# Reordering the slots of a software-pipelined attention and FFN kernel, and moving its last output step from VectorE to ScalarE and GpSimd

## The reference, cut to what matters

```python
# layer 1, per sequence
ifg = concat([q, k, v]); ig = ifg @ igate_w.T + igate_b; fg = ifg @ fgate_w.T + fgate_b
log_D = tril(cumsum(log_sigmoid(fg))[s] - cumsum(...)[t]) + ig[t]
D_mat = exp(log_D - max_t(log_D))
C = (q_h @ k_h.T / sqrt(16)) * D_mat
h = (C / (maximum(abs(C.sum()), exp(-max_log_D)) + 1e-6)) @ v_h
x1 = x + layernorm(h) * ln_scale
# layer 2
y = concat([n, -n]) with n = layernorm(x1)
out = x1 + s2 * (relu2(s1 * (relu2(s0 * (y @ W0)) @ W1)) @ W2)      # W: 128(256)->512->512->128, relu2 = 2*relu
```

## Time and profile before

| what | value |
|---|---|
| time before, median of 3 runs | 140.13 us (139.77 to 140.87) |
| the profiled execution's own time | 140.68 us |
| its span | 138.9 us |
| PE busy | 112.5 us, 81% |
| DVE busy | 95.9 us, 69% |
| ACT busy | 74.7 us, 54% |
| POOL busy | 70.0 us, 50% |
| mean granted TensorE clock | 0.956 of full |

### The profile page before, as it was taken

One profiled execution on the slowest core, in us unless ns is written; L12 is line 12 of the kernel. 1 busy time (PEld: TensorE's weight loads), 2 busy tenths in 40 slices (PEclk: granted clock), 3 DMA queues, 4 the chain that ended last, 5 costly groups with the idle time before them and its releaser, 6 DMA issues. The chain is left out here.

```text
span 138.9 us, 3358 instructions
## 1 busy us (share of the span) xinstructions
PE 112.5 (81%) x1141; PEld 83.7 (60%) x1141; DVE 95.9 (69%) x294; ACT 74.7 (54%) x173; POOL 70.0 (50%) x143
## 2 busy tenths in 40 slices
PE   4899999993998299979969698698888858769861
PEld 4777668562955185575827467376474656658751
DVE  5685595879689685809994994985898546471631
ACT  3026675974676464379649717835744631374230
POOL 5592675188784786654665777553214032520000
PEclk9999999999599959999999999999999977999997
DMA  3482190149683774635284753737001000101001
GB/s 104 138 224 49 39 258 15 42 60 183 121 151 61 161 132 66 134 54 101 19 189 76 156 105 88 147 38 159 2 5 38 0 5 0 38 0 38 17 26 38
DMA packets 12992, 11.38 MB, mean 82 GB/s; under 512 B 2080, under 2 KB 11440, under 8 KB 12976
## 3 DMA queue, kind: packets, MB, share of 16 engines
q0 software_dynamic: 1728, 6.29, 25.3%
q1 hardware_dynamic: 10112, 4.53, 12.7%
q10 hardware_dynamic: 1136, 0.35, 1.0%
HBM read 8.94 MB, written 1.25 MB: 73 GB/s over the span
## 5 line engine op out<-in xcount | busy, mean ns | idle before, releaser
L453 PE MATMUL pF<-h,w 128*128 128x256 f16 x256 | 31.1, 277 | 0.0
L643 ACT ACTIVATE h<-pF 128x512 f16<-128x512 f32 x32 | 18.1, 594 | 22.9 <-PE pF L453 22.9
L870 DVE SCALAR_TENSOR_TENSOR h<-pF,h 128x512 f16<-128x512 f32 x32 | 21.1, 681 | 9.5 <-ACT h L643 9.5
L453 PEld LDWEIGHTS pF<-h,w 128*128 128x128 f16 x256 | 25.1, 100 | 3.1
L1017 POOL TENSOR_SCALAR ve_hx<-mv_hx 128x2 f32<-128x2 f32 (+1 forms) x17 | 4.0, 236 | 32.8 <-DVE mv_hx L828 31.7
L783 DVE SCALAR_TENSOR_TENSOR cmat<-pS,dmat 128x1024 f32<-128x1024 f32 x15 | 18.2, 1216 | 2.1 <-PE pS L379 2.1
L379 PE MATMUL pS<-q_heads,qcT 64*128 64x512 f32 x64 | 18.1, 641 | 0.3 <-DVE cmat L783 0.3
L996 POOL TENSOR_SCALAR_AFFINE_SELECT maxb<-aT 128x1024 f32<-128x1024 f32 x12 | 13.2, 1102 | 4.4 <-ACT em L573 4.4
L412 PE MATMUL pX<-ident,x2p 128*128 128x128 f16 x32 | 4.4, 217 | 13.6 <-POOL x2p L1029 13.4
L796 DVE SCALAR_TENSOR_TENSOR den<-pO,em 128x8 f32<-128x8 f32 x16 | 2.6, 164 | 17.1 <-PE pO L400 17.1
L1018 POOL TENSOR_TENSOR rs_hx<-ve_hx,minus_half 128x2 f32<-128x2 f32 (+1 forms) x17 | 13.0, 766 | 1.4
(11 more groups left out here) (124 smaller groups left out, 211.5 us busy)
## 6 DMA issues: line engine op xcount, KB each, us to landing
maxb<-running_max POOLq DMA_DIRECT2D x12, 512.0 KB, 5.3
out<-outb SPq DMA_DIRECT2D x8, 128.0 KB, 1.8
xs<-in_x SPq DMA_DIRECT2D x3, 256.0 KB, 7.2
cs_in<-in_ctx SPq DMA_DIRECT2D x3, 256.0 KB, 7.6
q_heads<-qcT SPq DMA_DIRECT2D x24, 32.0 KB, 2.7
xs<-in_x SPq DMA_DIRECT2D x2, 128.0 KB, 3.2
cs_in<-in_ctx ACTq DMA_DIRECT2D x1, 256.0 KB, 3.7
k_in<-in_L_ffn_k SPq DMA_DIRECT2D x1, 256.0 KB, 3.8
```

Source lines behind the costliest of these rows:

```text
L453: last = pe.matmul(bank[:, u], w1[:, k, columns], h1[:, k, part], start=(k == 0 and part == 0), stop=(k == FT - 1 and part == 1))
L643: act.activation(hidden(f, m, 0), ffn_place(f, m), ACT.Relu).then_inc(ffn_high, 1)
L870: dve.scalar_tensor_tensor(out=hidden(f, m, 1), in0=ffn_place(f, m), scalar=0.0, in1=hidden(f, m, 0), op0=ALU.max, op1=ALU.subtract).then_ ...
```

## The change

It has these parts:

- PE's slot: `turn_o(n-1)` goes ahead of the early FFN stage, `turn_late_xn` behind it; `spread_never`/`spread_max` go ahead of `turn_x2`; `keep_busy` (slots 3 to 5) has two products in place of five and stands ahead of `turn_o`.
- POOL's slot: `x2_take_low(n-4)` stays first, `hx_scale(n-1)` follows it (so each scaling comes one slot later than before, and ahead of `place`), then `place`, `take_values`, and the new `add_out` in slots whose early stage is LAST.
- DVE's slot: only the first `low` of the late stages is ahead of `make_c`, the second is behind it; `residual` and `x_statistics` come right after, then the scans, `norm_q`, `x_moments`, and the normalizer chain in one piece. `norm_group(2)` goes from the end of slot 1 to the place ahead of its gate scans.
- The output: ACT scales the last product from PSUM into a new buffer `out_x` in SBUF, POOL adds x1 to it; DVE's instruction for it goes. PE's wait for the bank is on ACT's copy (`out_scaled`).
- SP waits for the first group of ctx and the second of x before it issues the loads of the third groups.

```diff
@@ sync
             load_ctx(1)
+            sp.wait_ge(ctx_loaded[0], 16)
+            sp.wait_ge(x_loaded[1], 16)
             load_x(2)
@@ tensor, ffn
-                        pe.wait_ge(out_ready, f_before + 1)
+                        pe.wait_ge(out_scaled, f_before + 1)
@@ tensor, slot
                     weigh(n - 1)
-                if 0 <= n - 4 < B:
-                    turn_x2(n - 4)
-                if k == 3 and g + 2 < NG:
-                    turn_late_xn(g + 2)
-                for f, m in early:
-                    ffn(f, m)
                 if 2 <= n + 1 < DIRECT:
                     spread_never(n + 1)
                     spread_max(n + 1, 0)
                     spread_max(n + 1, 1)
+                if 0 <= n - 4 < B:
+                    turn_x2(n - 4)
+                if 3 <= n <= FFN_LAG:
+                    pe.wait_ge(exp_ready, DIRECT)
+                    keep_busy(2)
                 if 0 <= n - 1 < B:
                     turn_o(n - 1)
+                for f, m in early:
+                    ffn(f, m)
+                if k == 3 and g + 2 < NG:
+                    turn_late_xn(g + 2)
                 for f, m in late:
                     ffn(f, m)
                 if n == 1:
                     turn_am(1)
-                if 3 <= n <= FFN_LAG:
-                    pe.wait_ge(exp_ready, DIRECT)
-                    keep_busy(5)
@@ scalar, high
+                act.wait_ge(ffn_sums, sums_to(f, m))
                 if m == LAST:
+                    if f >= 2:
+                        act.wait_ge(out_ready, f - 1)
+                    act.activation(out_x[:, f % 2].rearrange("p j d -> p (j d)"), ffn_place(f, m)[:, 0], ACT.Copy,
+                                   scale=s_work[:, 7:8]).then_inc(out_scaled, 1)
                     return
-
-                act.wait_ge(ffn_sums, sums_to(f, m))
@@ vector, low
                 if m == LAST:
-                    dve.wait_ge(ffn_sums, sums_to(f, m))
-                    if f >= 2:
-                        dve.wait_ge(out_stored[f % 2], 16 * (f // 2))
-                    dve.scalar_tensor_tensor(out=outb[...], in0=ffn_place(f, m)[:, 0], scalar=s_work[:, 7:8],
-                                             in1=x1[...], op0=ALU.mult, op1=ALU.add).then_inc(out_ready, 1)
                     return
@@ vector, slot
-                for f, m in before:
+                for f, m in before[:1]:
                     low(f, m)
                 if n < B:
                     make_c(n)
+                for f, m in before[1:]:
+                    low(f, m)
+                if behind_2:
+                    residual(n - 2)
+                    x_at = x_statistics(n - 2)
                 ...
                 if n == 1:
+                    norm_group(2)
                     gate_scans(1)
                 if prepare and k == 0 and n > 0:
                     gate_scans(g + 1)
-                if behind:
-                    at = normalizer_1(n - 1)
                 if n >= 2:
                     norm_q(n + 3 * GB - 2)
                 if behind_2:
-                    residual(n - 2)
+                    x_moments(n - 2, x_at)
                 if behind:
+                    at = normalizer_1(n - 1)
                     at = normalizer_2(n - 1, at)
-                if behind_2:
-                    x_at = x_statistics(n - 2)
-                if behind:
                     at = normalizer_3(n - 1, at)
-                if behind_2:
-                    x_moments(n - 2, x_at)
                 ...
-                if n == 1:
-                    norm_group(2)
@@ gpsimd
+            def add_out(f):
+                pool.wait_ge(out_scaled, f + 1)
+                if f >= 2:
+                    pool.wait_ge(out_stored[f % 2], 16 * (f // 2))
+                first = FG * f % XR
+                pool.tensor_tensor(outb[:, f % 2], out_x[:, f % 2], x1[:, first:first + FG], ALU.add).then_inc(out_ready, 1)
@@ gpsimd, slot
                     x2_take_low(n - 4)
+                if 0 <= n - 2 < B + 1:
+                    hx_scale(n - 1)
                 place(n + LEAD)
                 take_values(n + GB)
-                if 0 <= n - 1 < B + 1:
-                    hx_scale(n)
+                for f, m in ffn_of_slot(n)[0]:
+                    if m == LAST:
+                        add_out(f)
```

More of the change, by code:

```diff
@@ L147, in xattn_ffn @@
         outb = sb("outb", [128, 2, FG, D])
+        out_x = sb("out_x", [128, 2, FG, D])
         pG = ps("pG", [128, 4, S])
@@ L218, in xattn_ffn @@
         ffn_low = sem("ffn_low")
+        out_scaled = sem("out_scaled")
         out_ready = sem("out_ready")
```

## The result

| what | before | changed |
|---|---|---|
| median time | 140.12 us (139.77 to 140.87, 4 runs) | 133.11 us (132.38 to 134.69, 4 runs) |
| ratio to before, 95% interval | | 0.9476 [0.9406, 0.9546] |
| profiled execution, its span | 140.68, 138.9 us | 132.38, 130.6 us |
| PE, DVE, ACT, POOL busy | 112.5, 95.9, 74.7, 70.0 us | 108.5, 100.3, 78.0, 76.0 us |
| mean granted TensorE clock | 0.956 | 0.974 |

A forecast was written before the change was run, and what follows sets the result against it. A ring of waits over four engines, none full, was taken to set the slots' pace. Terms 0 - 2.5 - 3.3 + 0.85 = -4.95 us gave 135.2 us against 140.13, its own range 133.3 to 137 (overall 131.8 to 139.0).

The forecast's parts named there:

- The ring and PE's slot: Slots' loop of waits over four engines, 6.17 us around, goes; PE then allows 5.2 a slot against 5.66.
- The x2p wait: PE's wait at L412 for POOL's fp16 remainder, predicted to fall from 13.4 us to under 4.
- the 5.2 that was walked through from slot 6: PE's slot time: slot 6's 4.31 us adjusted for an early FFN stage, giving 5.2 for even and odd slots.
- The collision: DVE's residual meets POOL's affine_select on the shared port: 0.25 us a slot added while place runs, to slot 12.
- DVE's slack of 0.35 us a slot: Spare DVE time per slot, from 9.7 us of DVE work for two slots against PE's 10.4.
- Slots 0 to 9: Early savings bring slot 6 forward 3 us, later slots lose them: net 0, bounds -2 and +2.
- slots 7 and 8 gave back: The xn turn behind the early FFN stage delays x2T; PE waits 1.3 us, 1.5 to 2 lost in all.
- The tail and the end: From weighting sequence 15 to turning x2(15), 12.2 us for 15.5 (-3.3); the output step at the very end, +0.85.
- nothing collides: Rival: ACT's order costs nothing in slots 7 and 8, affine_select misses residual; another -2 and -1, 132.2 us; chance 0.18.
- ACT's order costs nothing in slots 7 and 8: Half of a rival: no loss there from the xn turn behind the early FFN stage, worth another -2 us.
- The new ring at the old pace: Rival: a POOL and DVE loop turns in 5.66 us, slots gain nothing, only the tail does; 137.7 us; chance 0.18.
- the lower clock: Rival: fewer keep_busy products leave the clock at 1.2 GHz through slots 3 to 8; up to 142.2 us; chance 0.07.

The follow-up runs named there:

- e2: The kernel before with one edit: PE's turn_o moved ahead of the early FFN stage; 134.3 us, ratio 0.9629.
- e4: The kernel before with two edits: turn_o ahead of the early FFN stage, and POOL's scaling one slot later; 130.11 us, ratio 0.9304.
- g2: The changed kernel with DVE's slot back in the old order (both low ahead of make_c, chains woven), turn_o still hoisted; 131.04 us, ratio 0.9356.
- f4: The changed kernel with the output step back on DVE, nothing of it on ACT and POOL; 132.7 us, ratio 0.9448.
- h1: The kernel before with only SP's two waits ahead of the third groups' loads added; 139.91 us, ratio 1.0035.
- f3: The changed kernel with turn_late_xn put back ahead of the early FFN stage; 131.46 us, ratio 0.9466.
- e1: The changed kernel without SP's two waits ahead of the third groups' loads; 133.98 us, ratio 0.9612.
- f1: The changed kernel with turn_o put back behind the early FFN stage; 131.73 us, ratio 0.9451.
- g3: The kernel before with POOL's later scaling, SP's waits, norm_group(2) ahead of its scans, and spread and keep_busy(2) at their new places; 124.64 us, ratio 0.8911.
- g1: The changed kernel with turn_o back behind the early FFN stage and DVE's slot back in the old order; 127.77 us, ratio 0.9071.
- f2: The kernel before with POOL's scaling one slot later and SP's two waits ahead of the third groups' loads; 124.68 us, ratio 0.8924.
- e3: The kernel before with one edit: POOL scales a slot later, behind the remainder and ahead of place; 124.22 us, ratio 0.8889.

## Why the prediction was right, and where it was off

**The ring and PE's slot: right.** The x2p wait fell from 13.4 to 1.7 us (under 4 was asked for), turn_o waits 0.33 us a time (0.3), and slots 11 to 15 take 5.20 us: the 5.2 that was walked through from slot 6. That number held in e2, e4 and g2 as well, four kernels with different surroundings, so it is PE's own list with turn_o right behind weigh.

**The collision: the failed term of the slots.** 0.25 us a slot was added while `place` runs, and 0.05 for DVE. The meetings came as expected:

```profile
70.83 1.09 POOL L994 TENSOR_SCALAR_AFFINE_SELECT maxb<-aT 128x1024 f32<-128x1024 f32 x1
71.31 0.76 DVE L852 SCALAR_TENSOR_TENSOR x<-hsc,rs_hx,xs 128x128 f32<-128x128 f32 x1
```

residual takes 0.76 us here and 0.33 alone (87.25 and 91.55 in the changed kernel's DVE timeline), and its mean over the 16 is 0.49. In slots 11 and 12 DVE lost time and PE none: they are as long (5.19 and 5.20) as 13 to 15, in which `place` no longer ran. What was sized as a cost there is only use of DVE's slack of 0.35 us a slot, which the prediction had itself worked out. Slot 10, at 5.58, is the exception. DVE comes late out of slot 9, where the meeting above stands, and PE waits 0.20 us for the second `low`, its only wait at L457. In f4 the meeting of slot 9 takes 0.48 us for 0.76, and slot 10 5.21; g2, whose DVE order has that `low` ahead of make_c, has 5.21 too. So a part of this 0.38 may be the collision's; no run tells it from the rest. Slots 10 to 15 gave 3.16 us for 2.5. The Trainium skill ("SBUF — State Buffer", the section on the two separate sides) describes a port pair that the two engines hold in turn; the stretched instruction, which ends 0.15 us behind the affine_select (0.14 in the earlier trace rows), agrees, and says nothing of the span when the stretched engine is not the bound.

**Slots 0 to 9: 0 forecast, -2.67 measured, the largest miss.** Two thirds of it, 1.77, were there at the first scores, where nothing was forecast, and belong to how the profiled execution of before happened to start (h1 above). It is a term of single executions and not of the change, and most of the 1.3 us by which the two profiles differ more than the medians can be this. The other 0.90 is a term of the change, and it comes from a slot that was not walked through. Counted from the first scores, the slots that were walked through came out as said. Slot 7 starts 56.43 - 53.23 - 1.77 = 1.43 us early, for which 1.5 was said, and slots 7 and 8 gave back 14.18 - 12.80 = 1.38 (1.5 to 2 said), by the mechanism named, the xn turn behind the early stage:

```profile
58.67 0.59 ACT L551 COPY qcT<-pG 128x512 f32<-128x512 f32 x1 [2.22 <-PE pG L320]
59.15 0.59 ACT L639 COPY x2T<-pX 128x512 f16<-128x512 f16 x1
59.89 1.03 PE L449 MATMUL pF<-x2T,w 128*128 128x256 f16 x8 [1.26 <-ACT x2T L639]
```

PE waits 1.26 us (1.3 said), and f3, which undoes it, has it no more. That leaves 0.05 at the scores of slot 9. The failing step is slot 9, which takes 5.62 us where it took 6.47: the ring was broken in it too, and the walk took off only the wait of slot 5 and those from slot 10 on. In before PE waited 1.34 us there for the remainder:

```profile
72.64 0.27 PE L412 MATMUL pX<-ident,x2p 128*128 128x128 f16 x2 [1.34 <-POOL x2p L1029]
```

In the changed kernel's profile the start of slot 7 is the sum of two misses, and so partly luck: slot 6 starts 2.02 us early (3 said) and loses 0.59 (1.5 said). Slot 5 ran there at a mean granted clock of 0.64. In e1, f1, f3 and f4, which keep DVE's new order, slot 6 starts 3.3 to 3.4 early, takes 6.41 us for 4.31, and slot 7 starts 1.2 to 1.3 early, all counted from the first scores. PE's wait for the `low` of (0,1) behind make_c is in each of them, as in e1:

```profile
52.98 1.48 PE L455 MATMUL pF<-h,w 128*128 128x256 f16 x12 [1.04 <-DVE h L868]
```

**The tail and the end: right.** 12.14 us against 12.2, with the clock full, and +0.81 against +0.85.

**The rivals.** The measured median, 133.11, lies 0.2 below the range of the forecast itself (133.3 to 137) and in that of "nothing collides", whose 132.2 us is nearer to it than 135.2. That rival was right in that the collisions cost PE little or nothing; its other half, that ACT's order costs nothing in slots 7 and 8, was wrong. So the time came out near that rival's by other terms than its own: the collision was held too dear, and slot 9's part of the ring was left out. The new ring at the old pace did not come, and the lower clock came in two slices and not through slots 3 to 8.

**What the prediction did not ask.** It named the wait for ACT's copy, 0.28 us, and took it as part of PE's slot. It never laid PE's slot out with the stage left ahead of turn_o, and so didn't see that of the two cuts one was free and the other cost half a microsecond a slot. It also let DVE's order and the output step pass because the sums fitted under 5.2. They do, but for slot 10; under 4.7 they don't. The parts as a ladder, each step one kernel further from the fastest:

| kernel | ratio | step from the line above |
|---|---|---|
| g3: POOL's order and the start's edits | 0.8911 | |
| g1: + output on ACT and POOL, + xn turn behind the early stage | 0.9071 | +0.016 |
| g2: + turn_o hoisted | 0.9356 | +0.029 |
| changed: + DVE's order | 0.9476 (another comparison) | +0.012 |

The steps do not simply add. Over g1, DVE's order alone costs 0.9451 - 0.9071 = 0.038 (f1, of another chip), the hoist alone 0.029 (g2), and both together 0.040 (changed, of another comparison): either one is enough to lose the slot of 4.7.

**Open.** What the DVE order costs with the hoist in place (changed against g2, of different chips, with touching intervals) is seen in the profiles between the scores of slots 0 and 10 (58.98 us for 58.27) and in slot 10 (5.58 for 5.21), and was not traced to one wait. How the 2.2 us between g3 and g1 divide between the output step and the xn turn was not tried apart on that base. Part of it was seen: the 0.36 us waits at the x2 turn, 0.8 at the end, and a wait for x2T in slot 7 of 1.25 us. That e1 is above the changed kernel while h1 and f2 show nothing for the same two waits is not explained either; the first comparison is between chips.

## What to carry to other kernels

When a wait goes round several engines, list every edge of the ring and cut the one whose move costs nothing, here a scaling that could come one slot later in POOL's list; then ask what the bounding engine's list takes with every other part left as it was. An instruction that needs another engine's copy of a product should not stand right behind that product: the stage that looked like delay in the ring covered the copy, and moving turn_o ahead of it cost 0.49 us in each full slot. Try the parts of such a change one at a time, because the smallest may be worth more than the whole: 124.2 us for two moved lines, 133.1 for all of it.

## What the runs showed of the hardware that was not expected

TensorE's products can run slower in the start while the granted clock reads full. In the profile of before four transposes took 1.06 us at 7.13 and 0.60 at 11.73, and the windows there say 1.00 for the clock (busy us, then the clock, as above):

```profile
7.00:9.00 2.00, 1.76 (x9) 1.36 (x8) 1.53 (x6) 0.96 (x2) 1.85 (x4) 1.00 0.93 249
9.00:11.00 2.00, 2.00 (x33) 1.73 (x36) 1.64 (x6) 0.00 (x0) 1.91 (x3) 1.00 0.53 152
```

In e3's profile the same window reads 0.57, and eight projections take 0.66 to 0.68 us in it; in before they take 0.66 at 9.90, at a reading of 1.00, and 0.39 at 10.96. So the duration of a known product tells more of the start than the reading does:

```profile
9.00:11.00 2.00, 1.92 (x33) 1.72 (x35) 1.64 (x6) 0.22 (x1) 1.91 (x3) 0.57 0.57 162
```

A DVE instruction was stretched to the end of a POOL instruction that only writes: the pair of xn took 0.97, 1.39, 1.42 and 1.32 us in the profiles of before, e3, g2 and h1, where it ended 0.07 to 0.14 us behind POOL's MEMSET of 128x1024, and 0.60 in the ten others, where it had started 0.45 us or more ahead of it.

By these two together a comparison of two single profiles is off by up to 3 us (14.0 to 17.0) at the first scores, so the starts of fixed instructions should be compared from the first scores on, and the start checked by the durations of one known product and of this pair.

POOL's add of 128x256 took 0.72 or 0.73 us in its last five instances and 0.84, 1.02 and 1.03 in the first three, which stand in slots where DVE is nearly full; the mean of 0.815 is near the forecast's 0.86. Why the first three are longer was not tested.
